# Pacing twelve scatters, splitting a routing pass, moving one weight load and adding dummy matmuls between the attention and the tree layers of a fused block

## The chip, the cores and the metric

The kernel runs on one core of a Trainium2 chip. The metric is the device time of one execution in microseconds. Each core has five engines that run their own instruction streams and meet at semaphores: TensorE (PE), VectorE (DVE), ScalarE (ACT), GpSimd (POOL) and SyncE (SP). SP and ACT issue plain DMAs, POOL issues the indirect ones (scatters and gathers by a list of rows). All of them run on the core's 16 DMA engines.

## What is computed

A gated block over x (4 batches of 512 tokens, 256 features), in float32. Cut to what matters:

```
attn(kv, q):   16 heads of 16, causal mask, softmax; out @ Wo.T + bo
tree(x):       cur = 0; 4 times: cur = 2*cur + 1 + (x . node_w[cur] + node_b[cur] >= 0)
               leaf = cur - 15;  relu(x @ w1[leaf] + b1[leaf]) @ w2[leaf] + b2[leaf]
ffn(x):        q, k, v = tree_q(x), tree_k(x), tree_v(x)
               softmax(q k^T / 16) @ v
x = x + tanh(g_xattn) * attn(ctx, layernorm(x))
x = x + tanh(g_ffn)   * ffn(layernorm(x))
```

Each of the three trees has 16 leaves with 256x64 and 64x256 weights; a token uses one leaf of each tree.

## The kernel before

**Attention (0 to 310 us).** For each batch b, 44 units of work go through the engines: PE forms scores twice (for the maxima, 20 units ahead, and for the exponentials), DVE takes the maxima, ACT the exponentials, PE multiplies with the values. PE and DVE loops count the units as n and k; other work of neighbouring batches is hung on fixed numbers of them (`NODE_AT`, `RANK_AT` and so on). After a batch's attention its rows are projected, added to X, normed again (XS), and PE makes the scores of all 45 tree nodes (`node_scores_pe`).

**Routing.** DVE turns node scores into leaves: `route(first, last, step)` works on tiles first to last of the 16 tiles of 128 tokens, in nine steps over the tree levels and one running sum (CUM) per tile; every step waits for the one before. In batch 3's loop, once batch 2's scores are there, it routes tiles 0 to 11 (batches 0 to 2) in one go; the ranks of tokens within leaves are then formed by PE (`early_ranks`, before exponential unit 37) and turned into row numbers POSI by DVE (`early_places`, semaphore `pos_ready` 1). Batch 3 goes through the same at the very end (`late_places`, `pos_ready` 2 for tree q and 3 for the others), and `leaf_list` writes which leaf each of the 31 slots of 128 rows per tree belongs to (`leaf_ready`).

**The last chain (310 to 352 us).** Batch 3's attention output is transposed (aot), projected (o), added to X; X is transposed (x2t), evacuated by ACT and DVE into XT, scored (n), routed and placed. PE runs dummy matmuls here, `hold(n)`, n matmuls of 128x512 in bf16 whose result nobody reads. Meanwhile SP loads the second weights, W2 of the three trees (lines 439 to 448, per tree 64 rows, 63 rows and one bias row), and POOL sends the normed rows XS to their places in DRAM: `scatter(s, t)`, one DMA of 128 rows for tree s and tile t. Tree q's tiles 0 to 11 go at `pos_ready` 1, tiles 12 to 15 at `pos_ready` 2, the trees k and v after `pos_ready` 3 and then by the pace of the tree layers.

**Tree layers (352 to 480 us).** 48 units of up to two slots (256 rows): SP loads the rows (`load_rows`, three units ahead; the first also needs `pos_ready` 3 and all 16 scatters of tree q), PE transposes them, DVE copies the leaf's W1, PE multiplies by W1, ACT applies relu, PE multiplies by W2, DVE copies the result to YS (a ring of four), SP stores it. All SP transfers stand in one queue, in program order. PE puts 10 and 6 dummy matmuls behind the transposes of units 0 and 1 (`WARM`). POOL then gathers rows back, and the last attention follows (480 to 551 us).

Batch and turn bookkeeping: banks ps_a and ps_d of PSUM are used in turns; `turn[what]` is the number of a use, `a_full`/`d_full` count those written by PE, `a_free`/`d_free` those emptied.

Of the kernel before, what the change touches and what calls it, by code (L numbers as in the profile page):

```python
# [11 lines left out]
P = 128  # L12
B, S, D = 4, 512, 256
# [61 lines left out]
def build(nc, x, ctxt, g_x, g_f, wq, bq, wk, bk, wv, bv, wo, bo, trees, out):  # L75
# [9 lines left out]
    with stack:  # L85
# [269 lines left out]
        def _(sp):  # L355
# [69 lines left out]
            for b in range(B):  # L425
                if b + 2 < B:
                    bounce_out(b + 2)
                if b + 3 < B:
                    load_ctx(b + 3)
                if b + 2 < B:  # L430
                    bounce_in(b + 2)
                    fill_rows(b + 1)
                if b == B - 2:

                    sp.wait_ge(exp_full, NU * NG * (B - 1))
                    for s in range(SETS):
                        sp.dma_start(W1[:, LEAVES * 2 * HID * s:LEAVES * 2 * HID * (s + 1)].rearrange("p (l n) -> p l n", l=LEAVES),
                                     trees[s][2].rearrange("l (p j) h -> p l (j h)", j=2)).then_inc(w1_in, 16)
            for s in range(SETS):
                if s == 0:  # L440
                    sp.wait_ge(exp_full, NU * NG * B)
                if s == 2:
# [3 lines left out]
                sp.dma_start(W2[s][HID + 1:P, :].rearrange("p (l d) -> p l d", l=LEAVES),  # L446
                             trees[s][4][:, 1:HID, :].rearrange("l h d -> h l d")).then_inc(w2_in[s], 16)
# [16 lines left out]
            for i in range(NP + GXR + 1):  # L464
                if i + LOAD_LEAD < NP:
                    load_rows(i + LOAD_LEAD)
                r = i - GXR - 1
                if r >= 0:
                    n = len(slots(r))
                    sp.wait_ge(y_free, r + 1)  # L470
                    sp.dma_start(ys_dram[r // PAIRS][rows(r), :].rearrange("(k p) d -> p k d", p=P),
                                 YS[:, r % YSR, 0:n, :]).then_inc(y_out[r % YSR], 16)
# [6 lines left out]
        def _(pool):  # L479
# [90 lines left out]
            pool.wait_ge(pos_ready, 1)  # L570
            for t in range(EARLY):
                scatter(0, t)
# [204 lines left out]
        def _(pe):  # L777
# [282 lines left out]

            pe.wait_ge(w1_in, 48)
            pe.wait_ge(leaf_ready, 1)
# [94 lines left out]
        def _(dve):  # L1157
# [243 lines left out]
            def route(first, last, step):  # L1401
# [21 lines left out]
                elif step < ROUTE_STEPS + last - first:  # L1423
# [6 lines left out]
                    if t == last - 1:  # L1430
# [102 lines left out]
            for b in range(B):  # L1533
                for k in range(NU * NG + (PV_LAG if b == B - 1 else 0)):
# [41 lines left out]
                    if b >= 2 and k == NODE_AT[b] + 2:  # L1576
                        evac_scores(b - 1)
                    if b == B - 1 and k == NODE_AT[b] + 3:
                        for step in range(ROUTE_STEPS + EARLY):
                            route(0, EARLY, step)  # L1580
# [110 lines left out]
```

## Time and profile before

| | us |
|---|---|
| median of 3 runs | 554.95 |
| lowest and highest | 552.87, 558.67 |
| the profiled execution, whole | 553.09 |
| its span, first to last instruction | 551.4 |

Busy time in that span: PE 447.4 us (81%), DVE 327.2 (59%), ACT 216.7 (39%), POOL 140.7 (26%). The page's slices show TensorE's granted clock and how busy DMA was; they are read with the stages above. Busy shares are means over stages that have different limits, so the stretch from 310 to 363 us is read by itself: there PE has almost nothing to do, and the order in which waits end decides.

### The profile page before, as it was taken

The page shows a single profiled execution, that of the slowest core. Times are in us where ns is not written, and L with a number is a line of the kernel's source. Part 1 is how long each engine was busy: PE and PEld are TensorE (multiplying, and loading weights), DVE is VectorE, ACT ScalarE, POOL GpSimd, SP SyncE. Part 2 cuts the span into 40 slices and gives each one's busy share as a digit, 9 for nine tenths or more (in the row PEclk, how much of TensorE's full clock was granted, in tenths as well). Part 3 has the DMA queues.
Part 4 walks back from the last instruction along what each step waited for, and adds up shares of the span by engine and source line. Part 5 has one row for each costly group of instructions (what it writes and reads, how often), then busy time and mean ns, then how long its engine had stood idle before and what let it go on. Part 6 is the DMA issues. An engine that isn't in the chain of part 4 may idle for free.

```text
span 551.4 us, 9451 instructions
## 1 busy us (share of the span) xinstructions
PE 447.4 (81%) x2883; PEld 278.3 (50%) x2883; DVE 327.2 (59%) x1005; ACT 216.7 (39%) x444; POOL 140.7 (26%) x167
## 2 busy tenths in 40 slices
PE   4868679889896898899788742188887899999998
PEld 3433325345543355445344431166676677766766
DVE  4877757786578855787675648523434334544432
ACT  3210235455343443355445400034555455443332
POOL 8510500500016000000000251642553343164400
PEclk9996989999999879999998985589999999999999
DMA  8753696229923097402500398748988888633211
GB/s 253 188 184 110 176 249 202 77 79 193 260 76 115 3 181 213 133 3 78 155 1 3 78 261 172 236 118 253 276 287 259 264 255 273 196 87 105 87 48 58
DMA packets 79368, 86.09 MB, mean 156 GB/s; under 512 B 6615, under 2 KB 74644, under 8 KB 79316
## 3 DMA queue, kind: packets, MB, share of 16 engines
q1 hardware_dynamic: 73239, 72.33, 47.6%
q0 software_dynamic: 5152, 12.95, 7.3%
q8 instruction: 25, 0.41, 0.3%
q10 hardware_dynamic: 928, 0.20, 0.2%
q14 instruction: 24, 0.20, 0.1%
HBM read 46.10 MB, written 39.06 MB: 154 GB/s over the span
## 4 chain that ended last, share of the span: by engine, by line
PE 59%; DVE 17%; issue 7%; SPq 6%; DMA 6%; ACT 2%; another core or an unknown queue 2%; ACTq 1%; DVEq 0%
PE ps_max L1101 5%; PE ps_exp L873 5%; PE ps_max L851 5%; PE ps_max L1130 4%; SPq L448 4%; PE ps_pv L890 4%; PE ps_a L1114 4%; PE ps_d L1114 4%; DMA QK<-MT 4%; DVE ps_max L1270 4%; PE ps_a L811 3%; PE ps_d L786 2%; PE ps_d L811 2%; PE ps_d L1152 2%; PE ps_a L1152 2%
## 5 line engine op out<-in xcount | busy, mean ns | idle before, releaser
L702 ACT ACTIVATE PT<-ps_exp 128x512 f32<-128x512 f32 (+1 forms) x176 | 94.3, 558 | 138.6 <-PE ps_exp L878 137.3
L1270 DVE CUSTOM_DVE_ANT_0 ps_max<-ps_max,maskw 128x384 f32<-128x384 f32 (+1 forms) x128 | 79.7, 634 | 41.3 <-PE ps_max L851 39.3
L565 POOL DMA_INDIRECT xs_dram<-XS,POSI x48 | 47.3, 986 | 188.0 <-issue 142.8
L851 PE MATMUL ps_max<-QK 96*128 96x128 bf16 (+3 forms) x256 | 67.7, 319 | 18.3 <-DVE MX L1270 11.1
L873 PE MATMUL ps_exp<-QK 99*128 99x512 bf16 (+3 forms) x256 | 66.4, 313 | 7.0 <-DMA QK<-MT 7.0
L890 PE MATMUL ps_pv<-PT,VA 128*32 128x128 f32 (+3 forms) x512 | 50.3, 469 | 0.0
L757 ACT ACTIVATE PT<-ps_max,B1T 64x128 f32<-64x128 f32 x93 | 33.7, 363 | 36.8 <-PE ps_max L1101 17.9
L873 PEld LDWEIGHTS ps_exp<-QK 99*128 99x128 bf16 x256 | 24.2, 101 | 45.6 <-ACT PT L702 17.0
L878 PE MATMUL ps_exp<-maskt,identb 128*128 128x128 bf16 (+2 forms) x176 | 44.3, 251 | 0.0
L851 PEld LDWEIGHTS ps_max<-QK 96*128 96x128 bf16 x256 | 22.4, 101 | 43.1 <-DVE MX L1270 19.4
L1273 DVE TENSOR_REDUCE MX<-ps_max 128x2 f32<-128x512 f32 (+1 forms) x48 | 32.3, 687 | 19.4 <-PE ps_max L855 19.3
L540 POOL TENSOR_TENSOR Q<-Q,PARTS 128x512 f32<-128x512 f32 x8 | 9.7, 1216 | 127.1 <-ACT PARTS L627 127.1
L1101 PE MATMUL ps_max<-PT 128*64 128x128 f32 x372 | 31.5, 283 | 12.1 <-issue 8.0
L1636 DVE COPY PARTS<-ps_a 128x512 f32<-128x512 f32 x24 | 16.6, 692 | 31.0 <-issue 24.7
L1636 DVE COPY PARTS<-ps_d 128x512 f32<-128x512 f32 (+1 forms) x24 | 15.8, 658 | 27.9 <-issue 22.5
L1101 PEld LDWEIGHTS ps_max<-PT 128*64 128x64 f32 x372 | 20.7, 136 | 19.4 <-issue 15.5
L1083 PE MATMUL ps_pv<-ident,Q 128*128 128x128 f32 x96 | 15.7, 287 | 17.6 <-DMA Q<-xs_dram 17.6
L1130 PE MATMUL ps_max<-QK 128*128 128x512 f32 x64 | 29.9, 592 | 0.0
L1622 DVE COPY PT<-QK 128x128 f32 x93 | 17.5, 232 | 20.2 <-PE ps_max L1101 14.6
L744 ACT ACTIVATE PT<-ps_pv 128x512 f32<-128x512 f32 x24 | 14.3, 597 | 36.9 <-issue 31.5
L765 ACT ACTIVATE Q<-ps_max,negm 128x512 f32<-128x512 f32 x16 | 11.0, 687 | 35.9 <-DVE negm L1642 34.6
L1083 PEld LDWEIGHTS ps_pv<-ident,Q 128*128 128x128 f32 x96 | 15.1, 202 | 19.0 <-issue 18.0
(225 smaller groups left out, 821.9 us busy)
## 6 DMA issues: line engine op xcount, KB each, us to landing
xs_dram<-zeros SPq DMA_DIRECT2D x12, 992.0 KB, 8.1
Q<-xs_dram SPq DMA_DIRECT2D x45, 256.0 KB
ys_dram<-PARTS SPq DMA_DIRECT2D x45, 256.0 KB
QK<-parts_dram SPq DMA_DIRECT2D x36, 256.0 KB, 7.6
parts_dram<-PARTS SPq DMA_DIRECT2D x16, 384.0 KB, 2.6
QK<-parts_dram SPq DMA_DIRECT2D x24, 128.0 KB, 2.8
X<-in_x_dram SPq DMA_DIRECT2D x4, 512.0 KB, 8.3
out_dram<-X SPq DMA_DIRECT2D x16, 128.0 KB
```

The lines of the kernel that those rows point to most:

```text
L565: nc.gpsimd.indirect_dma_start(out=xs_dram[s][:, :], out_offset=bass.IndirectOffsetOnAxis(ap=POSI[:, c:c + 1], axis=0), in_=XS[:, t, :], i ...
L702: nc.scalar.activation(PT[:, grp % 2, heads[0]:heads[-1] + 1, START[j]:START[j] + w], ps_exp[:, k % EXP_BANKS, 0:w * len(heads)].rearrange ...
L757: last = nc.scalar.activation(HT[0:HID, r % 2, k, :], ps_max[half, r % 2, 0:P], ACT.Relu, bias=B1T[half, bass.ds(leaf[k] + LEAVES * (j // ...
L851: last = nc.tensor.matmul(ps[:, a, :], q_of(b, HG * hg + h, ROWS, P * i, P * (i + 1)), k_of(b, HG * hg + h, ROWS, 0, w), start=(a == 0), s ...
L873: nc.tensor.matmul(ps_exp[:, k % EXP_BANKS, w * a:w * (a + 1)], k_of(b, HG * hg + h, ROWS_MAX, P * j, P * (j + 1)), q_of(b, HG * hg + h, R ...
L878: nc.tensor.matmul(ps[:, :, 0:P], identb[:, :], maskt[:, :].unsqueeze(1).to_broadcast([P, len(heads), P]), start=False, stop=True, skip_gr ...
L890: last = nc.tensor.matmul(ps_pv[STRIP * h:STRIP * (h + 1), P * j:S], VA[:, b % 2, j, VW * (HG * hg + h):VW * (HG * hg + h) + STRIP], PT[:, ...
L1101: last = nc.tensor.matmul(ps_max[HID * k:HID * (k + 1), r % 2, 0:P], W1S[:, r % 2, k, HID * a:HID * (a + 1)], GXS[:, r % GXSR, k, a, :], s ...
L1114: last = nc.tensor.matmul(ps_y(r)[:, D * k:D * (k + 1)], HT[:, r % 2, k, :], W2[j // SLOTS][:, bass.ds(leaf[r][k] * D, D)], start=True, st ...
L1130: last = nc.tensor.matmul(ps_max[:, n % 2, :], YT[:, b % 2, 0, k, P * t:P * (t + 1)], YT[:, b % 2, 1, k, :], start=(k == 0), stop=(k == KT ...
L1270: nc.vector.tensor_tensor_reduce(scores, scores, maskw[:, S - w:S], 1.0, LOWEST, ALU.add, ALU.max, MX[:, b % 2, hg, i, heads[0]:heads[0] + ...
L1636: nc.vector.tensor_copy(YS[:, r % YSR, 0:n, :].rearrange("p k d -> p (k d)"), ps_y(r)[:, 0:n * D]).then_inc(y_free, 1)
```

## The change

Four things are changed.

1. `scatter(0, t)` for t from 0 to 11 is no longer issued in one go. Before t = 2, 4, 5, 6, 7, 8 and 10 POOL waits for an event of the last chain: all exponential scores written; the last group of attention rows taken (t); ACT's copy of aot; DVE's addition from ps_a (o, 0), then from ps_d (o, 1); DVE's copy of the transposed X (x2t, 1); DVE's reading of the node scores (n).
2. Tiles 0 to 7 (batches 0 and 1) are routed one step per unit, from unit 6 of batch 3's loop to unit 22; tiles 8 to 11 where all twelve were.
3. The 63-row part of tree v's W2 (1008 KB) is no longer loaded with the rest but in the tree layers, at i = 16 (`PAIRS`) of SP's loop, between the load of unit 19 and the store of unit 11.
4. PE runs 10, 8, 8 and 6 more dummy matmuls, after `pos_ready` 2, after `pos_ready` 3, after `leaf_ready` and after the 16 scatters of tree q.

```diff
+            def other_rows(s):
+                sp.dma_start(W2[s][HID + 1:P, :].rearrange("p (l d) -> p l d", l=LEAVES),
+                             trees[s][4][:, 1:HID, :].rearrange("l h d -> h l d")).then_inc(w2_in[s], 16)
...
-                sp.dma_start(W2[s][HID + 1:P, :].rearrange("p (l d) -> p l d", l=LEAVES),
-                             trees[s][4][:, 1:HID, :].rearrange("l h d -> h l d")).then_inc(w2_in[s], 16)
+                if s < 2:
+                    other_rows(s)
...
+                if i == PAIRS:
+                    other_rows(2)
...
+            paced = {2: (exp_full, NU * NG * B), 4: (d_free, turn["t", B - 1, NG - 1] + 1),
+                     5: (a_free, turn["aot", B - 1, 0] + 1), 6: (a_free, turn["o", B - 1, 0] + 1),
+                     7: (d_free, turn["o", B - 1, 1] + 1), 8: (d_free, turn["x2t", B - 1, 1] + 1),
+                     10: (d_free, turn["n", B - 1, 0] + 1)}
             for t in range(EARLY):
+                if t in paced:
+                    pool.wait_ge(*paced[t])
                 scatter(0, t)
...
+            pe.wait_ge(pos_ready, 2)
+            hold(10)
+            pe.wait_ge(pos_ready, 3)
+            hold(8)
+            pe.wait_ge(leaf_ready, 1)
+            hold(8)
+            pe.wait_ge(xs_out[0], 16 * T)
+            hold(6)
             pe.wait_ge(w1_in, 48)
-            pe.wait_ge(leaf_ready, 1)
...
+                    if b == B - 1 and 6 <= k < 6 + ROUTE_STEPS + T // 2:
+                        route(0, T // 2, k - 6)
                     if b == B - 1 and k == NODE_AT[b] + 3:
-                        for step in range(ROUTE_STEPS + EARLY):
-                            route(0, EARLY, step)
+                        for step in range(ROUTE_STEPS + EARLY - T // 2):
+                            route(T // 2, EARLY, step)
```

On POOL, where tree q's scatters stand, the twelve were, with the four of batch 3 behind them:

```order
L565 DMA xs_dram<-XS,POSI 3968x256 [waits xs_zero0,pos_ready,xn_ready]
L565 DMA xs_dram<-XS,POSI 3968x256 x11
L565 DMA xs_dram<-XS,POSI 3968x256 [waits pos_ready,xn_ready]
L565 DMA xs_dram<-XS,POSI 3968x256 x3
L565 DMA xs_dram<-XS,POSI 3968x256 [waits xs_zero1,pos_ready]
```

and are now (the scatter is line 572):

```order
L572 DMA xs_dram<-XS,POSI 3968x256 [waits xs_zero0,pos_ready,xn_ready]
L572 DMA xs_dram<-XS,POSI 3968x256
L572 DMA xs_dram<-XS,POSI 3968x256 [waits exp_full]
L572 DMA xs_dram<-XS,POSI 3968x256
L572 DMA xs_dram<-XS,POSI 3968x256 [waits d_free]
L572 DMA xs_dram<-XS,POSI 3968x256 [waits a_free] x2
L572 DMA xs_dram<-XS,POSI 3968x256 [waits d_free] x2
L572 DMA xs_dram<-XS,POSI 3968x256
L572 DMA xs_dram<-XS,POSI 3968x256 [waits d_free]
L572 DMA xs_dram<-XS,POSI 3968x256
L572 DMA xs_dram<-XS,POSI 3968x256 [waits pos_ready,xn_ready]
```

No scatter moved past another; seven waits stand between them.

On SP, in the loop of the tree layers, now (Q is the ring that rows are loaded into, PARTS the ring YS, PT the W2 of tree v):

```order
L463 DMA Q<-xs_dram 128x2x256 [waits xt_full]
L441 DMA PT<-in_L_ffn_v_w_dram 63x16x256
L478 DMA ys_dram<-PARTS 128x2x256 [waits y_free]
L463 DMA Q<-xs_dram 128x2x256 [waits xt_full]
L478 DMA ys_dram<-PARTS 128x2x256 [waits y_free]
```

The 63-row load stood in the row after tree v's 64-row load, before the first load of rows; it is now in front of the store of unit 11 and the load of unit 20.

On DVE, inside batch 3's loop, where the routing of tiles 0 to 7 begins, now (L1290 and L1293 are the maxima, L1323 and L1324 the division of attention rows):

```order
L1324 TENSOR_TENSOR AT<-ps_d,rden 128x4x64 [waits chain_dve]
L1428 TENSOR_SCALAR Q<-SC 128x360 [waits parts_ready,d_free]
L1290 ISA ps_max,MX<-ps_max,maskw 128x384 [waits max_full,chain_dve]
L1290 ISA MX 128x1
L1431 COPY Q<-Q 128x24
L1290 ISA ps_max,MX<-ps_max,maskw 128x384 [waits max_full,chain_dve]
L1290 ISA MX 128x1
L1433 TENSOR_SCALAR Q<-Q 128x24
L1290 ISA ps_max,MX<-ps_max,maskw 128x512 [waits max_full,chain_dve]
```

The rows on Q are new here, one behind each unit's maximum; the pass over tiles 8 to 11, further on, is a third as wide (128x180 for 128x540) and has four running sums for twelve.

## Rows read from the trace of the kernel before

**Rows 1.** Chain that ended last: start us, length us, what; from 322 to 356 us.

```profile
322.10 8.67 SPq L448
...
335.01 9.52 SPq L448
344.53 7.89 issue
352.47 3.08 DMA Q<-xs_dram
```

**Rows 2.** Timeline, 321 to 334 us: start, us, engine, line, what [idle before <-releaser].

```profile
321.46 0.60 PE L786 MATMUL ps_d<-ident,X 128*128 128x128 f32 x4
...
326.10 0.60 ACT L615 ACTIVATE XT<-ps_a 128x512 f32<-128x512 f32 x1 [10.38 <-remote]
328.96 0.69 DVE L1218 COPY XT<-ps_d 128x512 f32<-128x512 f32 x1 [6.06 <-remote]
...
329.80 3.62 PE L944 MATMUL ps_d<-NODET,XT 128*128 128x45 f32 x16 [7.09 <-DVE XT L1218]
...
333.52 0.78 DVE L1340 SCALAR_TENSOR_TENSOR SC<-ps_d,y,SC 128x45 f32<-128x45 f32 x4 [1.20 <-PE ps_d L944]
```

**Rows 3.** Windows: length, busy us PE, PEld, DVE, ACT, POOL, clock, DMA share, GB/s.

```profile
312.00:320.00 8.00, 6.49 (x34) 4.86 (x35) 4.09 (x9) 1.19 (x2) 6.17 (x7) 1.00 1.04 239
...
322.00:328.00 6.00, 0.71 (x4) 0.10 (x1) 0.80 (x5) 0.60 (x1) 3.80 (x4) 0.94 1.00 277
...
338.00:344.00 6.00, 0.10 (x2) 0.00 (x0) 5.48 (x28) 0.00 (x0) 1.24 (x2) 0.50 0.64 120
```

**Rows 4.** Timeline, POOL's scatters and DVE's end of the last chain.

```profile
320.70 0.96 POOL L565 DMA_INDIRECT xs_dram<-XS,POSI  x1 [0.30 <-issue]
...
342.45 0.96 POOL L565 DMA_INDIRECT xs_dram<-XS,POSI  x1 [15.73 <-DVE POSI L1459]
...
346.42 1.90 POOL L565 DMA_INDIRECT xs_dram<-XS,POSI  x1 [0.30 <-issue]
...
351.15 0.24 DVE L1531 TENSOR_SCALAR MX<-AT 128x93 int32<-128x93 f32 x1
```

**Rows 5.** Timeline, the start of the tree layers on PE.

```profile
355.69 1.10 PE L1083 MATMUL ps_pv<-ident,Q 128*128 128x128 f32 x4 [17.60 <-DMA Q<-xs_dram]
...
356.59 4.47 PE L1090 MATMUL ps_exp<-onesb,identb 128*128 128x512 bf16 x10
...
361.55 1.46 PE L1090 MATMUL ps_exp<-onesb,identb 128*128 128x512 bf16 x6
...
362.94 0.66 PE L1101 MATMUL ps_max<-PT 128*64 128x128 f32 x8
```

**Rows 6.** Timeline, twelve tiles' routing and PE behind it; then batch 3's routing.

```profile
300.33 0.44 DVE L1408 TENSOR_SCALAR Q<-SC 128x540 bf16<-128x540 f32 x1
...
306.21 0.34 PE L957 MATMUL ps_max<-Q,trib 128*128 128x384 bf16 x1 [1.28 <-DVE Q L1428]
...
334.33 0.25 DVE L1408 TENSOR_SCALAR Q<-SC 128x180 bf16<-128x180 f32 x1
...
336.60 0.84 DVE L1428 TENSOR_TENSOR Q<-Q 128x48 bf16<-128x48 bf16 x4
```

**Rows 7.** Windows of batch 3's units and of the tree layers; columns as in rows 3.

```profile
270.00:280.00 10.00, 8.64 (x65) 5.98 (x66) 4.93 (x13) 3.66 (x7) 0.00 (x0) 1.00 0.01 2
280.00:290.00 10.00, 8.25 (x62) 3.33 (x63) 9.35 (x38) 4.79 (x10) 0.00 (x0) 1.00 0.01 2
...
385.00:410.00 25.00, 21.77 (x160) 17.46 (x160) 10.17 (x29) 13.40 (x32) 12.51 (x14) 1.00 0.90 283
...
460.00:480.00 20.00, 19.96 (x147) 15.95 (x143) 9.75 (x25) 11.11 (x26) 4.70 (x5) 1.00 0.72 223
```

**Rows 8.** Timeline: SP's store of unit 11, DVE's copy of unit 15.

```profile
398.05 0.47 SPq L471 DMA_DIRECT2D ys_dram<-PARTS  x1
...
406.35 0.42 DVE L1636 COPY PARTS<-ps_d 128x256 f32<-128x256 f32 x1 [1.80 <-issue]
```

More of the change, by code:

```diff
@@ L1429, in route @@
                                                       sel[:, w * t:w * (t + 1)], ALU.add)
-                    if t == last - 1:
+                    if t == last - 1 and last > T // 2:
                         ins.then_inc(sel_ready, 1)
```

## The prediction

> **What bounds the kernel now.** The change touches a stretch of 50 us and puts one transfer into the next stage, so I read three views there: the chain that ended last, the timeline, and windows. In the chain [rows 1] the path from 322 to 352 us is SP's: its bias-row issues last 8.67 and 9.52 us, since they stand behind 1 MB loads, and then SP waits 7.89 us for the sixteen scatters of tree q. The first load of rows goes out at 352.47 and ends PE's wait 3.08 us later. But the chain names only what ended last. Beside it runs DVE's chain to `leaf_ready` at 351.15 + 0.24 = 351.39 [rows 4], one microsecond ahead. Both have to come forward, or nothing does.
>
> DVE's chain holds a hole that no work explains [rows 2]. PE ends the transposes of X at 321.46 + 0.60 = 322.06; ACT's copy starts at 326.10, DVE's at 328.96, each released by something the profile calls "remote", and PE's node scores only at 329.80. Both engines wait for nothing but those transposes, so their semaphores were seen 4 to 7 us late. In that time DMA is full (share 1.00, 277 GB/s) and four scatters are issued [rows 3]. PE's clock falls to 1.2 GHz as well (0.50 in the last window of rows 3), so the 16 node matmuls take 3.62 us.
>
> **The last chain without the hole.** DVE is busy 0.80 us between 322 and 328 [rows 3], with small steps ahead of its copy; the copy could start at 322.9 and end 0.69 us later, at 323.6. PE then scores; no row has these 16 matmuls warm, at half the cold 3.62 us they end at 325.6. DVE meanwhile has the rest of its steps: between its copy's end (329.65) and 333.52 it waited 1.20 us, so the work is 2.7 us [rows 2], and it reads the scores at 326.3 against 333.52. Gain 7.2 us, if the hole goes. Everything behind on DVE is a chain of small steps of the same lengths. With the 0.5 us of the routing (below) all of it comes 7.7 us sooner: the first scatter of batch 3 (342.45) at 334.8, `leaf_ready` (351.39) at 343.7.
>
> **The pacing.** Before, POOL issued one scatter per 1.26 us; t = 7 went at 320.70 [rows 4]. Now t = 6 and 7 wait for the additions of o, which stand ahead of the transposes at 321.46 and so are over by then: they move little. Only t = 8 to 11 move: 8 and 9 from about 322 to 323.6, the end of DVE's copy, and 10, 11 to about 327.1, the end of its reading. The relief is small when the hole begins, but it limits itself: the four issues that fell into the hole [rows 3] can't go before DVE has its copy. The waits cost nothing: at 1.26 us each the twelve are out by 330, before batch 3's first at 334.8, and behind them on POOL stand only scatters. Bounds: the hole stays, 0 us gained; it goes, 7.2. Since the full DMA from 312 to 320 with seven scatters delayed nobody [rows 3], load alone isn't the cause; I take 7.2 as the likelier end, as the hole lies where four more scatters came on top of a queue that was already full.
>
> The Trainium skill's page SBUF — State Buffer, "Who interferes with whom", says that DMA never contends with a compute engine. By that rule the scatters aren't to blame, pacing gains 0, and the sum below loses its largest term; no row shows the port side of it, and what was late here were semaphores, of which the page doesn't speak. It is rival 1.
>
> **Routing sooner.** For tiles 8 to 11 routing takes what batch 3's takes: 334.33 to 337.44, 3.1 us [rows 6]. From 300.33 it ends at 303.4 instead of 306.2. PE waited 1.28 us for it [rows 6], and that is all it can get back. Against it stand 17 new steps of about 0.25 us in batch 3's loop. The first nine fall where DVE has room (busy 4.93 of 10 us at 270 to 280); the last eight, running sums of 0.21 us each (0.84 for four), where it is busy 9.35 of 10 [rows 6, 7], and can cost 1.7 us. Net between -1.3 and +1.7; I take -0.5.
>
> **The 63 rows, out of the gap.** In 338 to 344 us DMA runs at share 0.64 and 120 GB/s [rows 3]: that is this load alone, on part of the 16 engines. 1008 KB (1.03 MB) at 120 GB/s are 8.6 us. Without it SP's last bias issue, 9.52 us long from 335.01 [rows 1], ends near 337, and SP waits for the scatters only. They land when? Before, the last was issued 346.42 to 348.32 and SP was released at 352.47, 4.1 us later [rows 1, 4]. With scatters 7.7 us sooner the first load goes at 344.8, and its rows arrive at 347.9. This term of 7.7 holds the hole's 7.2 and the routing's 0.5; the 63 rows add none of their own, they only take SP out of the way (344.53 would be as late).
>
> The Trainium skill's page DMA: Bandwidth & Descriptors, section "Why a DMA increments its semaphore by 16 and not by 1", says that the number of engines is the largest up to 16 that divides the outer count: nine for 63 rows, 0.56 of the engines. By that rule the trace agrees (0.64, with scatters' and fetches' traffic in it), and the sum would be the same.
>
> **The clock.** Before, PE ran unit 0's transposes in 1.10 us cold, ten dummies in 4.47, six in 1.46, and reached the first W1 product at 362.94, 7.25 us after its rows [rows 5]. Warm, by the six, a dummy is 0.24 us (ten: 2.4) and four transposes are 0.60 [rows 2]: 0.60 + 2.4 + 0.60 + 1.46 = 5.1 us. The new dummies: 18 from about 334 on, 8 at `leaf_ready`, 6 at the last scatter's landing. Between the 18 and `leaf_ready` PE idles some 3 to 5 us. Before, it stopped at about 322.7 (0.71 us of work in the window) and the clock's mean of 0.94 over that window puts the fall at 327.3 [rows 3]: 4.6 us of idling is where it fell. If warm, the 14 take 343.7 to 347.0 and hide under the load (347.9); if cold, 14 x 0.447 = 6.3, to 350.0, and 2.1 us show, half of the time. Gain 2.15 - 1.05 = 1.1 us.
>
> **The 63 rows, in the tree layers.** SP issues them at i = 16, right ahead of the store of unit 11, which went at 398.05; behind that store stands the load of unit 20. DVE's copy of unit 15 (406.35) needs that store landed, since the ring has four places [rows 8]. With 8.6 us of transfer and 2 us to land it is there at 408.7: 2.3 us late. DMA is at share 0.90 there [rows 7], and scatters share the engines; if that stretches it by half (12.9 us) it is 6.6 us late. Against it: PE has slack here (21.77 of 25 us busy, 19.96 of 20 later), and DMA has room later (0.72 at 460 us) [rows 7]. Bounds: 0 (all absorbed) and 9; I take 3.
>
> **Sum**, against the profiled execution (553.09, span 551.4): -7.7 (first load) - 1.1 (clock) + 3 (tree layers) = -5.8, so 547.3. That execution lies 1.9 us under the median of 554.95; on the median the sum is 549.1. I say 549.
>
> **The rivals.**
> *Rival 1, the hole stays* (late semaphores that the pacing doesn't touch). `leaf_ready` then comes at 350.9. The last scatters land 0.5 us sooner by the routing and perhaps another 1, as W2 is through by then: 1.5. The 18 dummies run from 341 to 348 and leave PE warm: 2.1. The sum is -1.5 - 2.1 + 3 = -0.6: 554.3. For it: the twelve move little before 323 us. Against: the coincidence above. Chance 0.28.
> *Rival 2, slower*: the 63 rows stop the tree layers. Nine engines at 0.90 get 8.6 us of work more and everything that SP queued stands behind it; if scatters take every second turn it is 17.2 us, and if no slack takes it up, all of it shows: -8.8 + 17.2 = +8.4, 563.4. It decides from a cost of 8.8 us on, and from 14.3 for slower by over 1%. Against: between 398 and 406 us the units already loaded go on, and take up some of it. Chance 0.13.
> *Rival 3, the moved load is free*, since DMA's later room takes it up, and PE is warm throughout: -7.7 - 2.15 = -9.85: 545.1. Chance 0.1.
> *The forecast*: 0.49, own range 545 to 552.5.
>
> **Numbers.** About 1% (5.5 us) is what a measurement of this kernel can tell from no change; the three runs span 5.8 us. Faster by over 1% means under 549.4: 0.6 of the forecast's share, rival 3, and a little of rival 1, together 0.42. Slower means over 560.5: rival 2, 0.12 with what lies beside it. The rest, 0.46, is the same. The range 543.5 to 557 leaves out rival 2 and the edges.
>
> **What would show it.** Right: DVE's copy of XT within 1.5 us of the transposes, first load of rows at 344 to 346 us, first W1 product at 351 to 356, clock 1.00 in the dummies behind `leaf_ready`; the 63-row load issued near 390 us, and behind it DVE's copy of unit 15 late by 2 to 7 us. Wrong: a "remote" wait of over 3 us anywhere in 315 to 330 (rival 1), a stop of over 9 us about unit 16 (rival 2), or DVE maxima that PE waits for in 280 to 290 us.

## The result and the profile of the changed kernel

| | before | changed |
|---|---|---|
| median of 20 runs each, us | 551.79 | 548.16 |
| lowest and highest | 548.5, 558.67 | 543.3, 554.35 |
| the profiled execution, its span | 553.09, 551.4 | 546.43, 544.7 |
| clock over the span | 0.941 | 0.956 |

The ratio is 0.9927 with a 95% interval of 0.9899 to 0.9954: faster by 0.5 to 1.0%. Ratios come from the fast runs alone, here and below, and medians from all runs, so the two agree only roughly. The two profiled executions differ by 6.7 us, more than the medians (3.6), as one is above its median and the other below.

The hole of [rows 2] is gone. Timeline of the changed kernel (lines are 13 to 20 higher here: L799 was L786, L957 was L944, L1360 was L1340):

```profile
322.34 0.60 PE L799 MATMUL ps_d<-ident,X 128*128 128x128 f32 x4
...
322.54 0.60 ACT L628 ACTIVATE XT<-ps_a 128x512 f32<-128x512 f32 x1 [6.04 <-PE ps_a L799]
...
323.62 0.69 DVE L1238 COPY XT<-ps_d 128x512 f32<-128x512 f32 x1
...
324.46 1.95 PE L957 MATMUL ps_d<-NODET,XT 128*128 128x45 f32 x16 [0.88 <-DVE XT L1238]
...
327.02 0.78 DVE L1360 SCALAR_TENSOR_TENSOR SC<-ps_d,y,SC 128x45 f32<-128x45 f32 x4
```

From the transposes' end to DVE's copy it is 0.68 us (6.90 before), the 16 node matmuls take 1.95 us warm (3.62 cold), and DVE reads the scores at 327.02 instead of 333.52, 6.5 us sooner. The windows that answer those of rows 3 and 7 (same columns):

```profile
322.00:328.00 6.00, 3.54 (x27) 2.82 (x26) 5.41 (x29) 0.60 (x1) 2.88 (x3) 0.99 0.98 240
338.00:344.00 6.00, 2.68 (x12) 0.98 (x10) 5.97 (x4) 0.00 (x0) 4.78 (x5) 0.99 0.78 198
...
385.00:410.00 25.00, 19.86 (x135) 15.74 (x136) 8.89 (x26) 10.55 (x25) 11.38 (x12) 0.93 0.92 279
```

DMA is as full in 322 to 328 as before (0.98 for 1.00), but DVE works through it; in 385 to 410 PE does 1.9 us less than before. The chain that ended last runs no longer through SP, but through DVE's list of leaves and the dummies:

```profile
341.02 3.27 DVE AT L1548
...
344.95 4.83 PE ps_max L938 x14
349.79 0.46 PE ps_pv L1103 x4
350.25 2.16 PE ps_exp L1110 x10
352.41 0.47 PE ps_exp L1103 x4
352.87 1.29 PE ps_exp L1110 x6
354.17 0.59 PE ps_max L1121 x8
```

The first W1 product starts at 354.10, where it was 362.94 [rows 5]: 8.84 us sooner. Of these 2.2 are given back by the end of the tree layers. The timeline shows the place, DVE's copy of unit 15, which comes 48.28 us after the first W1 product (43.41 before):

```profile
389.86 0.43 SPq L441 DMA_DIRECT2D PT<-in_L_ffn_v_w_dram  x1
390.34 1.85 SPq L478 DMA_DIRECT2D ys_dram<-PARTS  x1
...
402.38 0.42 DVE L1658 COPY PARTS<-ps_d 128x256 f32<-128x256 f32 x1 [6.20 <-issue]
```

**Marks.** To compare runs whose attention ends earlier or later, three stretches are measured between starts of rows in each timeline: A, from the node scores of batch 2 (x16, 297.21 in the kernel before) to the last group's transposes (ps_d<-ident,OT x4, 312.90); G, the gap, from there to the first W1 product (362.94); T, the tree layers, from there to the first maxima of the last attention (x8, 479.87). Behind T the last attention takes 70.2 to 70.3 us in the profiles without remote waits (last column) and 71.5 to 72.3 in those with them.

| profile | paced | tiles 0 to 7 sooner | 63 rows | dummies | A | G | T | remote waits |
|---|---|---|---|---|---|---|---|---|
| before | no | no | gap | no | 15.69 | 50.04 | 116.93 | yes, hole |
| changed | yes | yes | moved | yes | 15.21 | 40.41 | 119.11 | yes, no hole |
| e1 | yes | no | gap | no | 17.87 | 50.19 | 112.53 | none |
| e2 | no | yes | moved | yes | 14.42 | 40.68 | 117.47 | none |
| e3 | no | no | moved | no | 17.88 | 43.11 | 117.92 | none |
| e4 | yes | no | moved | yes | 17.84 | 40.71 | 114.04 | none |
| e5 | yes | yes | moved | yes | 14.42 | 40.58 | 117.01 | none |
| e6 | yes | yes | gap | yes | 12.69 | 48.75 | 112.05 | none |
| e7 | no | no | moved | yes | 15.23 | 40.70 | 114.64 | none |
| e8 | no | no | gap, split | yes | 15.35 | 47.75 | 111.27 | none |
| e9 | no | no | gap | no | 19.19 | 49.46 | 116.80 | yes, hole |
| e10 | yes | yes | pieces | yes | 12.97 | 41.49 | 116.93 | yes, no hole |
| e11 | yes | yes | pieces | yes | 12.97 | 39.53 | 120.24 | yes, no hole |
| e12 | no | yes | pieces | yes | 16.82 | 48.19 | 119.80 | yes, hole |

"Remote waits" means waits of 1 us and more that the profile puts down to a remote releaser, anywhere in the trace. They stand in all profiles taken on some chips and in none taken on others, so two kinds of chips (or of conditions) have to be kept apart. e1 to e4 ran on one chip, e5 to e8 on another, e9 to e11 on a third, e12 on a fourth; on which the first pair ran is not known, but both show these waits. The kernel before is slower where they stand: medians of 556.22 and 554.17 us on the third and fourth chip, 549.51 and 548.8 on the first two.

A profile shows one execution, and not always a typical one. Those of e4, e7 and e8 (541.29, 540.9 and 542.05 us) are the fastest of their runs, 3.9, 4.4 and 6.9 us under the medians; that of e12 (559.86) is the slowest of its twelve, 4.8 us over its median.

Between the two first profiles G gives -9.63, T +2.18, the start of G +0.79 and the last attention -0.04: -6.70, the difference of the spans.

### The profile page after: what moved, and what is told of

It is laid out like the page before. It is cut to its first block, busy times and chain, and to the rows that moved or that the text cites. A ratio compares the mean times of both kernels' runs of the same rounds, so it can differ in the third digit from the quotient of the medians.

```text
span 544.7 us, 9532 instructions
## 1 busy us (share of the span) xinstructions
PE 454.1 (83%) x2915; PEld 279.5 (51%) x2915; DVE 327.8 (60%) x1014; ACT 216.4 (40%) x444; POOL 140.8 (26%) x167
## 4 chain that ended last, share of the span: by engine, by line
PE 64%; DVE 20%; issue 6%; DMA 5%; ACT 2%; another core or an unknown queue 1%; ACTq 1%; DVEq 0%; SPq 0%
PE ps_pv L903 6%; PE ps_max L1121 5%; PE ps_exp L886 5%; PE ps_max L864 5%; PE ps_max L1150 4%; PE ps_a L1134 4%; PE ps_d L1134 4%; DMA QK<-MT 4%; DVE ps_max L1290 4%; PE ps_a L824 3%; PE ps_d L799 3%; PE ps_d L824 2%; PE ps_d L1172 2%; PE ps_a L1172 2%; PE ps_a L799 2%
## 5 line engine op out<-in xcount | busy, mean ns | idle before, releaser
L1290 DVE CUSTOM_DVE_ANT_0 ps_max<-ps_max,maskw 128x384 f32<-128x384 f32 (+1 forms) x128 | 79.9, 634 | 40.9 <-PE ps_max L864 38.3
L1293 DVE TENSOR_REDUCE MX<-ps_max 128x2 f32<-128x512 f32 (+1 forms) x48 | 32.3, 687 | 17.4 <-PE ps_max L868 17.2
L605 POOL DMA_INDIRECT QK<-ys_dram,POSI x16 | 15.1, 945 | 26.0 <-PE ps_max L1150 20.6
L1134 PE MATMUL ps_d<-QK,PT 128*128 x60 | 18.2, 425 | 3.4 <-DVE PARTS L1658 3.4
```

Of the source, the lines that this page charges most:

```text
L1134: last = nc.tensor.matmul(ps_y(r)[:, D * k:D * (k + 1)], HT[:, r % 2, k, :], W2[j // SLOTS][:, bass.ds(leaf[r][k] * D, D)], start=True, st ...
L1290: nc.vector.tensor_tensor_reduce(scores, scores, maskw[:, S - w:S], 1.0, LOWEST, ALU.add, ALU.max, MX[:, b % 2, hg, i, heads[0]:heads[0] + ...
```

## The experiments

### e1 and e6: what the 63 rows hold up

e1 is the kernel before with the pacing alone (the seven waits of the diff).

> The kernel before with the seven waits between the twelve scatters and nothing else. Theory (the scatters on top of a full DMA queue make the hole): DVE's copy of XT starts within 1.5 us of the last transposes of X and no wait of ACT or DVE of over 3 us is put down to a remote releaser between 310 and 335 us. The 63 rows still stand in SP's queue, whose last bias issue ended at 344.53 before, so the first load of rows goes at 345 to 346 and the time falls by 5 to 7 us (ratio 0.987 to 0.991). Rival (late semaphores of another cause, which pacing does not touch): a wait of 4 us or more stays in that stretch, and the time falls by under 1 us.

Measured: ratio 1.0019 (0.9974 to 1.0065), 550.9 us for 549.51. No hole, and `leaf_ready` at 348.2, yet nothing gained. Since no profile on this chip shows a hole, paced or not, the time of e1 says nothing on what pacing is worth where there is one; its gap does say something. The timeline of e1:

```profile
350.44 11.42 SPq L458 DMA_DIRECT2D Q<-xs_dram  x5
...
360.37 1.10 PE L1089 MATMUL ps_pv<-ident,Q 128*128 128x128 f32 x4 [25.49 <-DMA Q<-xs_dram]
```

The load of unit 0 was issued at 350.44, and PE had its rows only at 360.37, 9.9 us later. G is 50.19, for 50.04 with the hole, so a gap without the hole is as long as one with it. e6 is the changed kernel with only the 63 rows put back:

```diff
-                if s < 2:
-                    other_rows(s)
+                sp.dma_start(W2[s][HID + 1:P, :] ...).then_inc(w2_in[s], 16)
...
-                if i == PAIRS:
-                    other_rows(2)
```

> The changed kernel with the 63 rows of tree v back among the other W2 loads, the other three edits kept. The prediction: without them in the gap nothing is gained there, so their return costs nothing at the first load and saves the 3 us in the tree layers: 3 us under the changed kernel. Theory now, from the run with pacing alone, where the first rows landed 9.9 us after their load was issued (3.1 before): on their engines the rows stand behind the 63-row transfer, which ends at 355 to 360 whatever leaf_ready does. Then PE's first transposes of unit 0 come 6 to 10 us later than in the changed kernel, DVE's copy of unit 15 loses its stop of 5 us, and the time is 1 to 5 us over that of the changed kernel, about that of the kernel before.

Measured: ratio 0.9924 (0.989 to 0.9958) beside 0.9852 (0.9809 to 0.9895) for the changed kernel on the same chip (e5): 3.45 us more by the medians. Its chain:

```profile
340.10 7.10 DMA xs_dram<-XS,POSI
347.27 9.09 DMA Q<-xs_dram
356.49 1.10 PE ps_pv L1096 x4
```

Again 9.1 us from the load's issue to its rows. G is 48.75 for 40.58, so the 63 rows in the gap cost 8.2 us of it: 6.5 by the later rows (PE's transposes 42.54 us after the last group's, for 36.02), and 1.65 because PE had waited 6.48 us and went on at 1.2 GHz. Out of the gap they cost T 5.0 (117.01 for 112.05). The expectation with the later landing held; the prediction's, that they add nothing to the gap, fell.

The four profiles with the 63 rows in the gap say it once more. In before, e9, e1 and e6 the load of unit 0 is issued 39.6, 40.2, 33.4 and 33.3 us after the last group's transposes, the first two with a hole; its rows are there after 42.7, 42.8, 43.2 and 42.4 us. So the date of the load does not move the rows, and by e6 against e5 what holds them is the 63-row transfer ahead of them.

### e2 and e12: the pacing

e2 is the changed kernel with the seven waits taken out, and nothing else.

> The changed kernel with the twelve scatters in one go, the other three edits kept. Theory: the hole of 5 to 7 us is back between the transposes of X and the node scores, leaf_ready comes at about 351, and the time is 4 to 6 us over that of the changed kernel (about that of the kernel before, or 1 to 2 above, since the 63 rows in the tree layers are still paid). Rival (the hole is not made by the scatters, or comes only in some executions): no hole, and a time within 1.5 us of the changed kernel.

Measured: ratio 0.9919 (0.9882 to 0.9956), 543.2 us. No hole, though the scatters go out in one row; on the hole the rival was right. Its timeline:

```profile
321.85 0.60 ACT L622 ACTIVATE XT<-ps_a 128x512 f32<-128x512 f32 x1 [5.95 <-PE ps_a L793]
321.97 0.96 POOL L572 DMA_INDIRECT xs_dram<-XS,POSI  x1 [0.30 <-issue]
...
323.14 0.69 DVE L1232 COPY XT<-ps_d 128x512 f32<-128x512 f32 x1
323.23 0.96 POOL L572 DMA_INDIRECT xs_dram<-XS,POSI  x1 [0.30 <-issue]
...
323.98 1.95 PE L951 MATMUL ps_d<-NODET,XT 128*128 128x45 f32 x16 [1.08 <-DVE XT L1232]
```

Here the theory of the prediction seemed dead: full DMA, scatters on top, and no late semaphore. But this chip shows no remote wait anywhere. So e12 asked again, by chance on a chip that has them: the changed kernel without pacing, and with the moved load in pieces (e10, below).

> The changed kernel with the moved load in eight pieces and the twelve scatters in one go. It looks at two things. First, the hole: both profiles of the kernel before that come from chips where some waits are put down to a remote releaser have it, the paced kernels on those chips don't, and on the two chips without such waits no kernel has it, paced or not. Theory: if this profile shows waits put down to a remote releaser elsewhere (in the tree layers or the last attention), it also shows the hole, and with the rows out of the gap it now counts: 45 to 49 us from the last group's transposes to the first W1 product for 41.5 with pacing. If it shows none of them, there is no hole and 40.4 to 41.5 us. Rival: remote waits elsewhere and no hole, that is, pacing had no part in it. Second, the pieces: from the first W1 product to the first maxima of the last attention it took 112.1 us with the rows in the gap and 114.0 to 117.9 with the load moved in one piece on the chips without such waits, 116.8 and 116.9 (in pieces) on the one with them. Theory: 111.5 to 113 (or 116 to 118 with such waits). Rival: pieces cost as much as the one load, 114 to 117.9 (or 119 and more).

Measured: ratio 1.0016 (0.9986 to 1.0045), 555.02 us for 554.17. There is no gain, where the changed kernel and its paced form with pieces (e10) have 0.7 to 1.5%. The hole is back, one step sooner in the chain, and two engines stop on it. Timeline of e12:

```profile
325.81 0.75 DVE L1337 SCALAR_TENSOR_TENSOR X<-ps_a,tg,X 128x512 f32<-128x512 f32 x1 [2.20 <-PE ps_a L925]
...
330.12 0.96 POOL L572 DMA_INDIRECT xs_dram<-XS,POSI  x1 [0.30 <-issue]
...
333.52 0.75 DVE L1337 SCALAR_TENSOR_TENSOR X<-ps_d,tg,X 128x512 f32<-128x512 f32 x1 [6.18 <-remote]
...
334.37 1.09 PE L793 MATMUL ps_a<-ident,X 128*128 128x128 f32 x4 [6.95 <-issue]
```

PE had ended the second half of o at 324.67 + 1.89 = 326.56; DVE took it at 333.52, 7.0 us late and 3.4 us after the last of the twelve scatters was issued (330.12). G is 48.19, where the paced kernels have 40.4 to 41.5. This profiled execution is the slowest of its runs, so its lengths may be on the long side; the ratio does not depend on it. e10 and e11, paced and on a chip with remote waits, have no such wait in this place. No paced kernel ran on the chip of e12, so that the missing gain is the pacing's, and not this chip's, is likely and not shown.

### e9: the hole in the kernel before

> The kernel before once more, for a second profile. From the last group's transposes (line 786) to the first W1 product (line 1101) it took 50.0 us in the first profile, with the hole; the run with the rows back in the gap took 48.75 without a hole and with the dummies, which are worth 2.4. Theory now (the 63 rows of tree v end where they end, and hide the hole): with or without a hole 50 to 52 us, and the rows of unit 0 land 6 us or more after their load if there is no hole (3.1 with it). Rival (the prediction: the hole is 7.2 us of the path): without a hole 42 to 44 us; with one 50.

Measured in one run: 556.79 us, with a hole and G 49.46. Its timeline (PE had ended the first transposes at 332.09):

```profile
332.13 0.60 ACT L615 ACTIVATE XT<-ps_a 128x512 f32<-128x512 f32 x1 [12.30 <-PE ps_a L786]
```

and its chain:

```profile
321.99 3.07 another core or an unknown queue
326.73 3.31 another core or an unknown queue
331.00 1.09 PE ps_a L786 x4
...
357.23 2.54 DMA Q<-xs_dram
```

Two waits of over 3 us for late semaphores this time, ahead of the transposes, and the rows land 2.5 us after their load. With the hole (50.04, 49.46) and without (50.19 in e1) G is the same: the 63 rows were a second, hidden end of the gap at almost the same place. Both sides of the expectation had about 50 us with a hole, so e9 alone does not decide between them; e1 and e6 do.

All three profiles with a hole share one thing that the ratios can't show: the last late semaphore comes soon after the last of the twelve scatters was issued. The kernel before and e9:

```profile
325.76 0.96 POOL L565 DMA_INDIRECT xs_dram<-XS,POSI  x1 [0.30 <-issue]
```

```profile
326.89 0.96 POOL L565 DMA_INDIRECT xs_dram<-XS,POSI  x1 [0.30 <-issue]
...
330.15 0.75 DVE L1323 SCALAR_TENSOR_TENSOR X<-ps_d,tg,X 128x512 f32<-128x512 f32 x1 [3.42 <-remote]
```

DVE goes on 3.2 us after the twelfth scatter before (328.96), 3.3 in e9 and 3.4 in e12. The same stands in the last attention, at a place that the change doesn't touch, in the changed kernel too:

```profile
484.43 1.96 PE L1172 MATMUL ps_a<-QK 128*128 128x256 f32 x8
...
488.14 0.95 POOL L605 DMA_INDIRECT QK<-ys_dram,POSI  x1 [0.30 <-issue]
...
491.16 0.48 DVE L1622 SCALAR_TENSOR_TENSOR X<-ps_a,rd,X 128x256 f32<-128x256 f32 x1 [5.76 <-remote]
```

PE had ended at 486.39, DVE saw it 4.8 us late and 3.0 us after the last of a row of gathers, and DMA was at share 0.31 (486 to 492). In e2, on a chip without remote waits, the same step follows PE by 0.1 us. So what the late semaphores go with is a row of indirect DMAs on POOL, and not a full DMA. Why they are late stays open.

### e3 and e7: the dummies

e3 is the kernel before with the moved load alone, e7 the same with the dummies.

> The kernel before with the 63 rows of tree v taken from the gap into the tree layers and nothing else. Theory (the prediction: it frees nothing while leaf_ready and the scatters are late, and costs 3 us in the tree layers): first load of rows between 350 and 352.5, DVE's copy of unit 15 late by 2 to 7 us, time 1 to 3 us over that of the kernel before. Rival A (tree layers have room, so the move is free): within 1 us of the kernel before. Rival B (the 63 rows make the hole, being part of the full DMA load): no wait of over 3 us put down to a remote releaser between 315 and 335 us, and a time 2 to 5 us under that of the kernel before.

> The kernel before with the moved load and the dummy matmuls, without pacing and early routing. Theory: these two edits are the whole gain: time within 1 us of the changed kernel, or up to 3 us under it (the run without pacing stood at 0.9919). Rival (pacing carries the gain, as predicted): 4 us or more over the changed kernel.

Measured: e3 0.9956 (0.9913 to 0.9999), e7 0.9939 (0.9902 to 0.9976), on different chips. Both have no hole. The theory of e3, that the move alone frees nothing, fell: G is 43.11 for 50.19 in e1 on the same chip, and the time 2.8 us under the kernel before by the medians (546.68 for 549.51), though T grew by 5.4. In e3 PE takes the rows cold:

```profile
351.49 1.10 PE L1090 MATMUL ps_pv<-ident,Q 128*128 128x128 f32 x4 [18.02 <-DMA Q<-xs_dram]
...
352.38 4.47 PE L1097 MATMUL ps_exp<-onesb,identb 128*128 128x512 bf16 x10
```

and in e7 warm:

```profile
344.75 4.88 PE L932 MATMUL ps_max<-onesb,identb 128*128 128x512 bf16 x14 [3.96 <-DVE MX L1545]
...
349.69 0.72 PE L1097 MATMUL ps_pv<-ident,Q 128*128 128x128 f32 x4
...
350.24 2.32 PE L1104 MATMUL ps_exp<-onesb,identb 128*128 128x512 bf16 x10
```

G is 43.11 without and 40.70 with dummies: 2.4 us. It is all at the matmuls behind the rows: from unit 0's transposes to the first W1 product e3 takes 7.12 us and e7 4.56. The 14 dummies took 4.88 us, cold for the first part, and put nothing in front: PE's transposes begin 36.1 us after the last group's in e7, and 36.0 in e3. e7's ratio bears out the moved load and the dummies as a gain of 0.2 to 1.0% where there are no late semaphores. But these two edits were to be the whole gain, within 1 us, and e7 is 2.4 us over the changed kernel on its chip (545.3 for 542.9, e5). Its gap is the same (40.70 for 40.58), so pacing and early routing may be worth something outside the gap; with six runs of e5 it is not clear of noise. As for the hole, e3's rival B (the 63 rows make the hole) is not told apart, since that chip has none.

### e4: the routing

e4 is the changed kernel with tiles 0 to 11 routed in one pass.

> The changed kernel with tiles 0 to 11 routed in one pass, as before. The prediction gave the early routing -0.5 us (bounds -1.3 to +1.7). The trace of the changed kernel shows the last group of attention rows on DVE 0.8 us later than before. Theory now (early routing gains nothing, for the last chain starts later by it): time within 0.8 us of the changed kernel, or up to 0.8 under it, with the addition of the last group 0.5 to 1 us sooner. Rival (the forecast's gain is real): 0.5 to 1.3 us over it.

Measured: ratio 0.9955 (0.9922 to 0.9988), 545.19 us, with e2 at 0.9919 beside it. The changed kernel itself did not run on this chip, so neither side of the expectation can be read from the time. The routing moves more than 0.8 us, in both directions. Timeline of e4:

```profile
305.68 0.50 PE L970 MATMUL ps_max<-Q,trib 128*128 128x384 bf16 x1 [2.81 <-DVE Q L1448]
...
307.05 1.06 PE L799 MATMUL ps_d<-ident,OT 128*128 128x128 f32 x4
```

and of the changed kernel:

```profile
306.06 0.32 PE L970 MATMUL ps_max<-Q,trib 128*128 128x384 bf16 x1
...
307.18 0.66 PE L799 MATMUL ps_d<-ident,OT 128*128 128x128 f32 x4 [0.24 <-ACT OT L682]
```

PE waits 1.28 to 2.82 us in all seven profiles with one pass, and 0 in the seven with two; in four of the former (e1, e3, e4, e9) it waits over 2.8 us and goes on at 1.2 GHz, with 1.06 us for four transposes that take 0.60 to 0.66 warm (e3, e4, e9; the trace of e1 has only three of them). The other three (before, e7, e8) wait 1.28 to 1.37 us, and there the clock had been down shortly before the wait (0.50 in 302 to 304 of e7, 1.00 in 306 to 308), which lets PE come later to it. A is 15.2 to 19.2 us with one pass (mean 17.0) and 12.7 to 16.8 with two (mean 14.2). But the node scores of batch 2, where A begins, come at 297.5 in the mean of seven with one pass and at 300.2 with two. Measured from the node scores of batch 1 it is 49.6 to 50.6 us with one pass (mean 50.1) and 51.9 to 53.1 with two (52.5), without overlap: the 17 steps among the units cost PE 2.3 us. Part of it is PE's waits for DVE's maxima, 0.84 us in one before and 2.09 in three, at 283 to 287, in the changed kernel. The last group's transposes start at 314.5 and 314.4 in the mean, and at anything from 311.0 to 318.2. So it is a wash within what these profiles can tell; three of the seven with one pass are the fastest executions of their kernels, and chips are not the same. The times lean the other way: the kernels with one pass lie over those with two on both chips without remote waits (e4 2.0 us over e2, e7 2.4 over e5). Each of these pairs differs in the pacing as well and none is clear of noise, so whether early routing gains nothing or some 2 us stays open.

### e8: 48 and 15 rows for 63

The kernel before with the dummies, and with the 63-row loads cut in two:

```diff
-                sp.dma_start(W2[s][HID + 1:P, :] ... trees[s][4][:, 1:HID, :] ...).then_inc(w2_in[s], 16)
+                for lo, hi in ((HID + 1, HID + 49), (HID + 49, P)):
+                    sp.dma_start(W2[s][lo:hi, :] ... trees[s][4][:, lo - HID:hi - HID, :] ...).then_inc(w2_in[s], 16)
```

> The kernel before with the dummy matmuls, and with each tree's 63-row load cut into one of 48 rows and one of 15, all in the gap as before; nothing is moved, paced or routed sooner. Theory (63 rows run on part of the engines only, DMA share 0.64 for them alone, and that is why they last until the rows of unit 0 are due): the W2 loads are through before 345, the rows land within 4 us of their load, unit 0's transposes begin at 348 to 351 and the tree layers have no stop of 5 us: 3 to 7 us under the changed kernel. Rival (the 48 and 15 rows spread no wider, or total bytes decide): rows land 6 us or more after their load, time that of the kernel before.

Measured: ratio 1.0012 (0.9972 to 1.0052). The rival was right: windows of 312 to 344 us, first e6 (rows whole, in the gap), then e8:

```profile
312.00:344.00 32.00, 18.86 (x109) 11.00 (x101) 26.51 (x90) 2.39 (x5) 18.03 (x18) 0.84 0.90 222
```

```profile
312.00:344.00 32.00, 17.79 (x85) 10.43 (x85) 25.82 (x84) 1.19 (x2) 18.90 (x19) 0.81 1.12 230
```

The DMA share is higher (1.12 for 0.90) and hardly more is moved (230 for 222 GB/s). The last scatter now lands 9.2 us after its issue (7.1 in e6), the rows 6.2 after theirs (9.1), which is 41.6 us after the last group's transposes (42.4), and G is 47.75 for 48.75. The share fits a transfer that was spread wider, and the time fits bytes that decide; the two profiles also differ in the pacing and the routing, so bytes are the likelier limit and not shown.

### e10 and e11: the load in pieces, and no dummies behind the rows

e10 is the changed kernel with the moved load cut by leaves, `other_rows(2, l, 2)` loading 63 rows of leaves l and l + 1:

```diff
-                if i == PAIRS:
-                    other_rows(2)
+                if i % 2 and 3 <= i < 3 + LEAVES:
+                    other_rows(2, i - 3, 2)
```

and e11 the same with `WARM = {}`.

> The changed kernel with the moved load cut by leaves into eight pieces of 63 rows x 2 leaves, issued one at a time at every second pass of the loop from i = 3 to i = 17. Theory (the one 1008 KB piece stops the stores and loads queued behind it: the chain of the changed kernel shows a store landing 14.3 us after its issue at 386.8): no store lands over 6 us after its issue on the chain between 380 and 410 us, no wait of PE for PARTS of over 2 us there, and 2 to 4 us under the changed kernel (ratio to the kernel before 0.978 to 0.988). Rival (bytes decide, DMA being at 0.9, not the piece): same stop spread out, time within 1 us of the changed kernel.

> The same, without the 10 and 6 dummy matmuls behind the transposes of units 0 and 1 (they take 2.32 and 1.46 us on a warm PE, right on the path from unit 0's rows to the first W1 product). Theory (the dummies ahead of the rows have warmed PE, so these are pure length now): first W1 product 3 to 3.8 us sooner from the last group's transposes, 37 us for 40.6, clock 1.00 from 350 on, and 2 to 3.5 us under the run with the pieces alone. Rival (PE falls back to 1.2 GHz in the waits of the first units, or the units wait for something else): clock under 0.9 in 350 to 370, or the gain is given back by unit 5; time within 1 us.

Measured on one chip: e10 0.9869 (0.9786 to 0.9952), e11 0.988 (0.9792 to 0.9968), 546.01 and 546.19 us for 556.22, from six runs each. Both are faster than the kernel before; how they stand to the changed kernel, which did not run here, is open. The stop of the one-piece load is gone: the longest wait of DVE's copies in 380 to 410 is 3.11 us, where it is 6.20 to 8.70 in the six profiles with one piece. The windows of 390 to 400 us show it, first e5 (one piece):

```profile
390.00:400.00 10.00, 5.82 (x46) 4.53 (x44) 1.32 (x6) 4.26 (x10) 5.73 (x6) 0.91 0.93 282
```

where the chain of e5 has a store of 14 us,

```profile
386.77 14.27 DMA ys_dram<-PARTS
```

then e10:

```profile
390.00:400.00 10.00, 7.92 (x58) 6.27 (x57) 3.59 (x12) 4.28 (x11) 5.29 (x6) 1.00 0.91 302
```

PE does 2.1 us more in them. T of e10 (116.93) is that of the kernel before on chips with remote waits (116.93, 116.80), so the pieces look free there; e12, with the same pieces, has 119.80 in its slowest execution, outside the 116 to 118 expected. That pieces are better than one load is likely, and not settled: no run has both on one chip. In e11 the first W1 product came 2.0 us sooner (G 39.53 for 41.49), not 3 to 3.8, and T was 3.3 longer:

```profile
350.57 0.74 PE L1103 MATMUL ps_exp<-ident,Q 128*128 128x128 f32 x4 [0.56 <-DMA Q<-xs_dram]
...
352.37 0.66 PE L1121 MATMUL ps_max<-PT 128*64 128x128 f32 x8 [1.06 <-ACT PT L757]
```

PE waited for rows and ACT instead of running dummies, and later fell back in clock (0.83 in 360 to 370). The rival of that run held.

### e5: the changed kernel again

> The changed kernel once more, with a profile of its own, as the measure for the runs beside it. In the first four runs a wait put down to a remote releaser between 310 and 335 us was in no profile, with or without pacing, so the hole is suspected to be an accident of some executions. Theory: no hole here either, ratio to the kernel before 0.989 to 0.995. Rival: the hole shows here too, about 6 us long, and the time of the profiled execution is above the median.

Measured: ratio 0.9852 (0.9809 to 0.9895), 542.9 us for 548.8; no hole, G 40.58.

## Why the prediction came out

The time was right (549.0 said, 548.16 measured), and so was the place of the gain. Part of that is luck. The 549 starts from 554.95, the median of three runs, and the median of twenty is 551.79: of the 5.95 us said, 3.6 came by the medians, and the base was 3.2 too high. The profiled pair (-5.8 said, -6.7 measured) is nearer, but its two executions lie on either side of their medians. One step behind the time was wrong as well, and its error did not show, since the change held both parts.

- **"What bounds the kernel now": right on two ends, blind to a third.** SP's end and `leaf_ready` were read as the two that have to come forward. The third was the landing of the rows behind the 63-row transfer. It can't be read as a wait in [rows 1], where the load was issued at 352.47 and landed 3.08 us later: by then the transfer was through.
- **The hole, 7.2 us: size right, the condition half right.** The scores were read 6.5 us sooner, DVE's copy came at 323.62 (323.6 said), the node matmuls took 1.95 (1.8 said; that no row has them warm was a slip, batch 2's at 297.21 in the kernel before take 1.95). On chips with remote waits the hole goes with the pacing: unpaced before, e9 and e12 have it, paced changed, e10 and e11 don't. That is a pattern over six profiles, and no pair on one chip differs in the pacing alone. In the gap of the two chips without remote waits pacing is worth nothing (G 40.68 and 40.70 without, 40.71 and 40.58 with). That the DMA was full, which the forecast took for half of the cause, is not needed: in the last attention the same waits come at a share of 0.31. The Trainium skill's page SBUF — State Buffer, section "Who interferes with whom", says that DMA never contends with a compute engine; that pacing then gains 0 agrees with the gaps of e2 and e5 and not with e12. What was late was a semaphore, and the port side is shown by no run.
- **"The 63 rows add none of their own": wrong.** This is the step that failed. By it the hole alone would have been worth 7.2 us of the gap, and moving the load nothing. But with the 63 rows in the gap it is as long without the hole as with it (e1 50.19; 50.04, 49.46), and the 63 rows alone hold 8.2 us of it (e6 against e5); moving them without pacing took 7.1 us off the gap where there is no hole (e3 against e1), and the rest without pacing gained nothing where there is one (e12, 1.0016). Two ends of almost equal date stood beside each other, and each hid the other.
- **The scatters' landing.** 344.8 was said for the first load, 346.14 came. The last scatter went at 339.92, 6.5 us before that of [rows 4], and took 4.3 us from its end to the load, as before (4.1).
- **The clock, 1.1 us said, 2.4 measured** (e3 against e7). PE was warm or nearly so when the rows came; the 14 dummies took 4.83 to 4.88 us, between the 3.3 warm and 6.3 cold, and ended about when the rows arrived (a load at 346.14 and the 3.1 us of before give 349.2, PE went on at 349.79), so at most 0.6 of the 2.1 us showed.
- **The routing, -0.5 said: -0.5 in the means of the marks (-2.8 in A, +2.3 ahead of it), but of two parts that both lie outside the bounds, and perhaps 2 us by the times.** The gain was said to be at most 1.28, the wait of one profile; the wait reaches 2.82 in others, and PE goes on at 1.2 GHz behind it. The cost was bounded at 1.7. One of the signs of being wrong, PE waiting for DVE's maxima in 280 to 290, came true (2.09 us for 0.84). That the parts cancel as said is luck.
- **The 63 rows in the tree layers, +3 said: 2.2 between the first pair, 4.3 on the two chips without remote waits** (mean T 116.2 in five profiles, 112.0 in three with the rows in the gap). The copy of unit 15 came 4.9 us later behind the first W1 product (48.28 for 43.41), in the 2 to 7 said. As said, later work takes part of it back.
- **Rival 1** (the hole stays, 554.3) was wrong for the kernel, and comes near for its unpaced form, e12 (1.0016; 0.999 by the rival). **Rival 2** didn't come: no stop went over 9 us, though the copy's wait reached 8.70 in e5. **Rival 3** (545.1, moved load free) is what e10 aimed at.
- The page DMA: Bandwidth & Descriptors of the Trainium skill, section "Why a DMA increments its semaphore by 16 and not by 1", gave nine engines for 63 rows. By it 48 rows take sixteen and 15 rows fifteen. With these two the share rose from 0.90 to 1.12, which agrees; the throughput did not follow.

## What to carry to other kernels

When a wait goes away, ask for every transfer that is queued ahead of the next one needed when it ends, not only for those that the chain names; two ends of equal date hide each other, and taking away either alone can measure as nothing. Test such a pair with both halves, each alone and each left out. And look at several executions on more than one chip before a wait is called structural or accidental, and run both halves of a pair on the same one. Three runs are a thin base for a forecast: here they were 3.2 us off.

## What the runs showed of the hardware

- Semaphores of PE were seen by DVE and ACT up to 7.0 us late while POOL issued a row of indirect DMAs: 4.0 and 6.9 us in the hole of [rows 2], 2.4 and 5.6 in e9, 7.0 in e12, and 4.8 in the last attention of the changed kernel. The last of them came 3.0 to 3.4 us after the row's last issue. The first three were at full DMA, the fourth at share 0.31. On two chips it never came, at the same load (1.00 and 292 GB/s in 320 to 328 of e2). The profile calls the releaser remote. With the twelve scatters spaced by the chain's own events there was no such wait among them in three profiles. What makes the chips differ stays open.
- Behind a wait of 2.81 us or more PE went on at 1.2 GHz (four transposes 1.06 us in e3, e4 and e9); behind one of 1.28 to 1.37 at 2.4 GHz (0.60 in e7 and e8).
- The same bytes in loads of 48 and 15 rows for 63 gave DMA share 1.12 for 0.90, and 230 for 222 GB/s.
- One 1008 KB load held the 256 KB stores behind it for 12 to 14 us from issue to landing (11.71 in e7, 14.27 in e5); cut into eight of 126 KB, the copies that need these stores waited 3.11 us at most (e10).
